# A hand-planned order of steps for a four-layer gated block, laid out anew around the value products and scores of three attentions

## The chip, the cores and the metric

The kernel runs on one core of one Trainium2 chip. The metric is the device time of one execution in microseconds; lower is better.

## The reference

Sixteen sequences of 256 tokens with 256 features pass through four layers. Each layer adds a gated cross- or self-attention and a gated feed-forward part to x; every part reads a layer-normalised x:

```python
x = x + jnp.tanh(g_xattn[0]) * _L0_xattn_ref(_layernorm(x, axis=-1), ctx_1024, ...)
x = x + jnp.tanh(g_ffn[0]) * _L0_ffn_ref(_layernorm(x, axis=-1), ...)
x = x + jnp.tanh(g_xattn[1]) * _L1_xattn_ref(ctx_1024, _layernorm(x, axis=-1), mask_BxS2_bk1, ...)
x = x + jnp.tanh(g_ffn[1]) * _L1_ffn_ref(_layernorm(x, axis=-1), ...)
...
```

The attentions that matter here are the one of layer 0 (32 score heads of width 8, two of them sharing one value head of width 16), the one of layer 2 (16 heads of width 16) and a third one inside the feed-forward part of layer 2 (16 heads of width 8). All three have this form:

```python
scores = jnp.einsum('bhtd,bhsd->bhts', q * scaling, k)
attn_w = jax.nn.softmax(scores.astype(jnp.float32), axis=-1).astype(scores.dtype)
...
attn = jnp.einsum('bhts,bhse->bhte', attn_w, v)
```

The rest: layer 0's feed-forward part applies three cycles of a small coupling network, each cycle reading the result of the one before it; layer 1 has a masked attention with 8 heads of width 64 over 512 keys and a mixture of ten experts; layer 2's mixture has eight experts; layer 3 has a one-head attention and a quantised two-matrix feed-forward.

## The kernel before

**Work.** Two sequences are in flight at a time, one in each of two slots of buffers (`SLOTS = 2`), so the 16 sequences take 8 passes. For each sequence the work is cut into named steps: `l0.q` is the query projection of layer 0, `l0.max`, `l0.exp` and `l0.pv` are parts of its attention, `f0` is the feed-forward part of layer 0, `f2` that of layer 2, and so on. A step has a part on some of the engines: TensorE fills a tile in PSUM, and ScalarE or VectorE reads it.

**An attention of the spread kind (layers l0, l2 and f2).** A unit is two heads. For unit u,
- `max` (line 625): TensorE computes scores, four matmuls that contract over 32 rows (64 in l2) of the array; VectorE takes their maximum (line 1243);
- when all units of the sequence have a maximum, `peak` and `shift` put the negated maxima into extra rows of the queries (line 558 on TensorE, line 1262 on VectorE);
- `exp` (line 642): TensorE computes the scores again, transposed and shifted, and ScalarE takes the exponential (line 975) into one of two buffers `pt_spread` of the slot (`EXPS = 2`), so ScalarE must wait until the value product two units back has read its buffer;
- `pv` (line 709): TensorE multiplies values by these probabilities. Each head writes 32 output rows and so uses 32 columns of the array, chosen by `tile_position=(0, g)`. The profile shows eight matmuls for a `pv` step, since each product in f32 runs as two.
- after every second unit (each item) ScalarE copies the result out of its bank `o` (line 913), and after four items TensorE transposes them back (`back`, line 721).

Which quarter of the array a unit uses follows from its number. In l0 and f2 an even unit's scores use rows 0 to 63 and an odd unit's rows 64 to 127, with the parity swapped in the odd slot (`u ^ (s % 2)`); a unit's value product uses the lower or the upper 64 columns in the same way. Two adjacent steps of one kind with different halves are called complementary below. In l2 a unit's scores use both halves of the rows, and only the value products have halves.

**PSUM.** Six banks are handed round (`placed_in_banks`) to all steps but `pv`, in the order of the steps; `max` and `exp` take two each, so only three such tiles are alive at a time. `take` makes TensorE wait until the step that held the banks last was read. Two further banks hold the value products.

**The order.** A single list of steps, `SCHEDULE`, sets the order on TensorE, VectorE, ScalarE and GpSimd alike: each of them walks the list and does its parts. The list is written out by hand as a string: every letter of `ORDER` names one of 24 lists (12 for each slot) of which the next step is to be taken, and each list keeps the right order among its own steps.

```python
lists = [iter([step for p in range(PASSES) for step in lists_of(p * SLOTS + n // LISTS)[n % LISTS]]) for n in range(LISTS * SLOTS)]
found = [next(lists[int(n, 36)], None) for n in ORDER]
return [step for step in found if step]
```

A step that comes too early in this list blocks its engine, since engines don't overtake; one that comes late delays what needs it. The feed-forward part f0 is a chain within a sequence: `t` (line 769 on TensorE) gives the coupling, VectorE's `turn` (line 1320) applies it, and `cT` (line 558) transposes the result for the next cycle.

Of the kernel before, what the change touches and what calls it, by code (L numbers as in the profile page):

```python
# [214 lines left out]
def lists_of(s):  # L215
# [14 lines left out]


ORDER = (
    "DAM11ADM11ADDAAMAAAA7AAAJAMAAAAAAAMA1AMMAMAD0M050M50M505M0M50M50M50M5M0550M50M50M5M0M505M0M55CC5HC0HCHCHCHCHC2H0CH0CHHC0"
    "HCHCHCH0CHC60HHE2607H606C002JC0C0C00CI0CIC00IC0CI0EC00CC200C0CC0CEC0C0C0CBC0EB0B0C00C5B0B0C500550B0C55B00CC5CB0N0C50NCC5"
    "NCCNHCNCHCNCHCC5H0HCNN007CHCCHHC3H0H0C30C093009C08980C968689C6CCCL6LCKIC8K6LCKLKL0I9KI08I9CIL068C9J09860L83698660CCKLKCI"
    "LI0KK0LII0KIC00F0C0FF00FC00000C00C00C505AC0C50C50C5C0C50C5C5C5C07C0CCHC0HCH0H00C0000CH00HC000C0H0H0H00C0JAC00055CCC0CCCC"
    "C05CC05C0C5C0C50C5C5CC4C57C04CC0HC0H0C0HCMHCHCHC0HHH0BCJ1CCGCC0G9DCB1CC8L0K69BCLI809K6CLI8BK60CI9LB8K069BC8L069KI8B6CI01"
    "L91K8BIA069CL8AA6K0ACILMADAK0D0ICDJA0ADA0AM0C7AA0MM1C0AA0CAC0AAAAA0AAM0C0MC0M50M50C505050M5CM0M50M50MCM550M50M50M50M5MMM"
    "CM050MCCC55HCH5C0HCHCHC2HCHCHC0HHCH0C7HC0HCHCH06C2EH6H06HC060002C0CC000C0ICIC00IC0CI00E0C00J2C0ECC0CCC0C0C0CBC0E0B0CB0CB"
    "C0500B500C550B0C55B00CC5CB00NC50NCC5NCCNHCNCH5CCHH70HCNCN0CCHCNCH0HC3H0H0CJ03C30F09090C898096C68869CCCLC6LCKCKL8KIL0I9IK"  # L240
# [32 lines left out]
    "C505C05C0C50C5C0C50C5C5C57C0C00CCHCHCH0C000000H00CH0C000HCH0H0H0JC00C00C055C0CCCCCC05CC05C0C5CC05C0C5CC5C45C0CC0H0CH0CHC"
    "H0CHCHCHHJ0H0CCGCCC0G9CCC8LK0I6C9L8K0C69I8LKC06IL9K8IC6L0K98CI60LK9I80C69L8K069I7CL8604KI0C00C0C0CC00CC0C0C0CC0C"
)


# [1561 lines left out]
```

How the kernel before makes its waits and increments, by code:

```python
        def full(eng, step, s, u=0):  # L479
            eng.wait_ge(S["s_wfull"], UNIT[step, s, u])
            return bank_of(step, s, u)
# [63 lines left out]
            def take(step, s, u=0):  # L546
                for last in BANKS[step, s, u][2]:
                    pe.wait_ge(*after(READ[last[0]], READER.get(last[0], last[0]), *last[1:]))
                return bank_of(step, s, u)
# [37 lines left out]
            def spread_attention(plan, what, s, u):  # L588
                st = plan.name
                if what in ("k", "q"):
                    act = ctxT[s] if what == "k" and plan is not F2 else x0T[s] if plan is L0 else xnT[s]
                    if what == "k" and plan is not F2:
                        pe.wait_ge(*after("s_ctxT", "ctxT", s))
                    else:
                        pe.wait_ge(*after("s_xnT", st + ".xT", s))
                    weight = mat({"l0": "l0_w", "l2": "l2_w", "f2": "f2_"}[st] + what, FC)
# [2 lines left out]
                    act, name = (xnT[s], "f2_v") if plan is F2 else (ctxT[s], st + "_wv")  # L599
                    filled(by_tokens(take(st + ".v", s), act, mat(name, FC), P if plan is F2 else D, FC))
                elif what in ("ks", "qs"):
                    w = take(st + "." + what, s, u)
                    pe.wait_ge(*after("s_lo", st + "." + what[0], s))
                    pe.wait_ge(s_select, 1)
                    sel = {32: {"q": sel8q, "k": sel8k}, 64: {"q": sel16q, "k": sel16k}}[plan.rows][what[0]]
# [301 lines left out]
        @block.scalar  # L908
        def _(act):
            act.wait_ge(s_first, 16)
```

## Time and profile before

| | |
|---|---|
| median of 3 runs | 4502.43 us (4487.78 to 4503.43) |
| span of the profiled execution | 4493.2 us |
| TensorE matmul busy | 4197.2 us (93%) |
| VectorE busy | 2949.1 us (66%) |
| ScalarE busy | 2085.8 us (46%) |
| mean granted TensorE clock | 0.972 |

The span runs from the first to the last instruction of the program in one profiled execution. No separate time of that execution is recorded beside its span; what lies around the span is taken as the difference to the median, 9.2 us. The profile's busy share of an engine counts the time in which at least one of its instructions runs.

### The profile page before, as it was taken

To read this page: it belongs to the slowest core of one execution; us is meant where nothing else is said; L and a number is where in the kernel's file an instruction comes from. 1 tells how busy PE (TensorE), PEld (TensorE's weight loads), DVE (VectorE), ACT (ScalarE), POOL (GpSimd) and SP (SyncE) were. 2 spreads that over 40 slices of the span, in tenths; PEclk is the share of its full clock that TensorE was granted. 3 is DMA by queue.
4 is the path that set the end of the run, shared out by engine and by line. 5 is a ranking of instruction groups with operands and counts; after the bars stand their busy time and mean duration, and the time that the engine had idled before them with its cause. 6 is when DMAs were issued, how large, how long until landed. Compare 5 with 4: busy or idle time off the path is not lost.

```text
span 4493.2 us, 73928 instructions
## 1 busy us (share of the span) xinstructions
PE 4197.2 (93%) x28256; PEld 3198.6 (71%) x28256; DVE 2949.1 (66%) x7812; ACT 2085.8 (46%) x3424; POOL 91.9 (2%) x180
## 2 busy tenths in 40 slices
PE   7898998989989899898999999999999999999998
PEld 4675966759667596675966759667696676956768
DVE  6667776676656666666765767657676576665655
ACT  4544455353553435535355353553535535356342
POOL 0000000000000000000000000000000000000000
PEclk8999999999999999999999999999999999999999
DMA  2010610103001030010300103001030010300012
GB/s 99 1 45 10 217 37 1 52 23 132 29 15 41 24 128 29 15 41 29 123 29 15 41 29 123 29 15 41 29 123 29 15 41 29 123 29 15 31 55 102
DMA packets 51769, 228.06 MB, mean 51 GB/s; under 512 B 4832, under 2 KB 21216, under 8 KB 31584
## 3 DMA queue, kind: packets, MB, share of 16 engines
q1 hardware_dynamic: 51424, 223.33, 13.8%
q8 instruction: 232, 3.80, 0.3%
q14 instruction: 113, 0.93, 0.1%
HBM read 202.34 MB, written 20.97 MB: 50 GB/s over the span
## 4 chain that ended last, share of the span: by engine, by line
PE 80%; DVE 12%; ACT 5%; issue 3%; DMA 0%; SPq 0%; DVEq 0%; ACTq 0%
PE w L574 18%; PE w L584 12%; PE o L709 11%; PE w L830 8%; PE w L820 8%; PE w L642 4%; PE w L558 4%; PE o L702 3%; DVE mx L1243 3%; PE w L625 3%; PE w L677 2%; PE w L567 2%; PE w L721 1%; DVE nt L1184 1%; PE w L612 1%
## 5 line engine op out<-in xcount | busy, mean ns | idle before, releaser
L1243 DVE TENSOR_REDUCE mx<-w 128x4 f32<-128x1024 f32 x512 | 606.8, 1221 | 180.5 <-PE w L625 167.2
L975 ACT ACTIVATE pt_spread<-w 128x1024 f32<-128x1024 f32 x512 | 519.9, 1024 | 236.8 <-PE w L642 203.7
L709 PE MATMUL o<-pt_spread,va 128*32 128x256 f32 x4096 | 543.2, 396 | 30.5 <-ACT pt_spread L975 29.8
L921 ACT ACTIVATE oth<-w,res 128x256 f32<-128x256 f32 x656 | 276.9, 471 | 569.4 <-PE w L820 470.3
L574 PE MATMUL w<-xnT,stream 128*128 128x256 f32 x1792 | 413.1, 382 | 1.4 <-ACT xnT L913 0.8
L574 PEld LDWEIGHTS w<-xnT,stream 128*128 128x128 f32 x1792 | 338.2, 191 | 50.7 <-DVE x L1212 1.0
L709 PEld LDWEIGHTS o<-pt_spread,va 128*32 128x32 f32 x4096 | 205.0, 111 | 202.2 <-issue 63.3
L820 PE MATMUL w<-qodd,va_hi 128*128 128x256 f32 x2048 | 344.8, 283 | 1.1 <-issue 0.8
L820 PEld LDWEIGHTS w<-qodd,va_hi 128*128 128x128 f32 x2048 | 284.6, 188 | 7.8 <-issue 2.4
L1502 DVE TENSOR_REDUCE mx<-w 128x2 f32<-128x1024 f32 x128 | 155.8, 1225 | 199.2 <-PE w L679 198.9
L1212 DVE SCALAR_TENSOR_TENSOR x<-w,gate,x 128x256 f32<-128x256 f32 x512 | 223.2, 477 | 90.6 <-PE w L830 71.7
L642 PEld LDWEIGHTS w<-qsp,ksp 32*128 32x128 f32 (+1 forms) x2048 | 151.0, 187 | 173.7 <-issue 139.7
L625 PE MATMUL w<-ksp,qsp 32*128 32x256 f32 (+1 forms) x2048 | 232.6, 339 | 36.3 <-DVE mx L1243 17.7
L642 PE MATMUL w<-qsp,ksp 32*128 32x256 f32 (+1 forms) x2048 | 245.5, 328 | 20.3 <-DVE qsp L1262 18.3
L702 PE MATMUL o<-pt,va 128*65 128x256 f32 x1024 | 238.8, 379 | 0.1
L625 PEld LDWEIGHTS w<-ksp,qsp 32*128 32x128 f32 (+1 forms) x2048 | 147.0, 197 | 124.1 <-issue 57.2
L574 PE MATMUL w<-xnT,res 128*128 128x256 f32 x768 | 211.6, 419 | 18.9 <-ACT xnT L913 14.5
L913 ACT ACTIVATE oth<-o 128x256 f32<-128x256 f32 (+1 forms) x384 | 146.7, 382 | 169.0 <-PE o L709 92.9
L820 PE MATMUL w<-qodd,stream_lo 128*128 128x256 f32 x1024 | 204.8, 282 | 0.0
L1084 ACT ACTIVATE oth<-w 128x256 f32<-128x256 f32 x160 | 61.3, 383 | 303.0 <-PE w L574 287.6
L1184 DVE SCALAR_TENSOR_TENSOR nt<-rs,ve 128x1 f32<-128x1 f32 x1056 | 184.5, 216 | 18.8
L913 ACT ACTIVATE pt<-w 128x1024 f32<-128x1024 f32 (+1 forms) x144 | 140.6, 976 | 113.2 <-PE w L567 95.6
(263 smaller groups left out, 7722.5 us busy)
## 6 DMA issues: line engine op xcount, KB each, us to landing
stream_lo<-split SPq DMA_DIRECT2D x56, 1024.0 KB, 4.8
va_hi<-split SPq DMA_DIRECT2D x56, 1024.0 KB, 6.9
stream<-in_moe_dram SPq DMA_DIRECT2D x80, 384.0 KB, 3.1
stream<-in_resident_dram SPq DMA_DIRECT2D x8, 2048.0 KB, 7.4
raw<-in_moe_dram SPq DMA_DIRECT2D x8, 1024.0 KB, 6.8
split<-va_hi SPq DMA_DIRECT2D x8, 1024.0 KB, 8.9
split<-stream_lo SPq DMA_DIRECT2D x8, 1024.0 KB, 10.8
stream<-in_resident_dram SPq DMA_DIRECT2D x8, 1024.0 KB, 4.7
```

The lines of the kernel that those rows point to most:

```text
L574: mm = pe.matmul(w[:, col0 + j * T:col0 + j * T + T], weight[:, k, (m0 + j) * P:(m0 + j + 1) * P], act[:, k, :], start=(k == 0), stop=(k = ...
L584: mm = pe.matmul(w[:, o:o + n], act[:, k, tt * P:(tt + 1) * P], weight[:, k, :], start=(k == 0), stop=(k == kc - 1))
L625: mm = pe.matmul(w[:, a * 512 + tt * T:a * 512 + (tt + 1) * T], qsp[s][b:b + plan.rows, c, tt * P:(tt + 1) * P], ksp[s][b:b + plan.rows, c ...
L642: mm = pe.matmul(w[:, a * 512 + kt * T:a * 512 + (kt + 1) * T], ksp[s][b:b + plan.rows, c, kt * P:(kt + 1) * P], qsp[s][b:b + plan.rows, c ...
L702: mm = pe.matmul(o[0:L1_DIM + 1, 0:T], by_heads1(s)[:, kt, u, :], p[:, kt * T:(kt + 1) * T], start=(kt == 0), stop=(kt == KT - 1))
L709: mm = pe.matmul(o[g:g + 32, 0:T], by_heads(plan, s)[:, kt, plan.v_of(h), :], p[:, a * 512 + kt * T:a * 512 + (kt + 1) * T], start=(kt == ...
L820: mm = pe.matmul(w[:, j * T:(j + 1) * T], wt[:, k, j * P:(j + 1) * P], a[:, k, :], start=(n == 0), stop=(n == len(parts) - 1))
L830: mm = pe.matmul(w[:, tt * D:(tt + 1) * D], a[:, k, tt * P:(tt + 1) * P], wt[:, k, :], start=(n == 0), stop=(n == len(parts) - 1))
L913: act.activation(out_ap, in_ap, ACT.Copy).then_inc(S[sig], 1)
L921: h = act.activation(dst[:, c, :], w[:, c * T:(c + 1) * T], func, bias=bias[:, c:c + 1], **more)
L975: act.activation(exp_buffer(plan.name + ".exp", s, u), w[:, :], ACT.Exp, scale=scale).then_inc(S["s_P"], 1)
L1243: dve.tensor_reduce(mx[s][:, :, 2 * v:2 * v + 2].rearrange("p t a -> p a t"), w[:, :].rearrange("p (a t k) -> p a t k", a=2, t=TT), AX_X, ...
```

## The change

Only the string `ORDER` changes. It has the same letters, each as often as before (5032), so the same steps are done with the same instructions, and each list keeps its own order; 1476 of the steps keep their place in the common list, the others move by 2 places on average (mean of all). The banks are handed round in the new order, so a step may get other banks and wait for another step's reader.

```diff
 ORDER = (
-    "DAM11ADM11ADDAAMAAAA7AAAJAMAAAAAAAMA1AMMAMAD0M050M50M505M0M50M50M50M5M0550M50M50M5M0M505M0M55CC5HC0HCHCHCHCHC2H0CH0CHHC0"
+    "DAM11ADM11ADDAAMAAAA7AAAJAMAAAAAAAMA1AMAADM0M0M50M50M50M50M50M50M50M5M0550M50M50M50M5500MMM55CC5HCHCHC0HCHCHC0HH2CC0HHH0"
...
```

Counted over the list of TensorE's 3856 steps, with the halves as defined above:

| | before | after |
|---|---|---|
| adjacent complementary value products, in pairs | 26 | 125 |
| adjacent complementary scores (l0, f2), in pairs | 175 | 252 |
| neighbours of different kind (32-row score, 64-row score, value product, any other) | 1740 | 1535 |

The 99 new value pairs lie in l0 (35), l2 (37) and f2 (27).

The first place is on TensorE in the third pass, in layer 0 of the odd slot (`va1`), about the middle of its 16 units; `ob0` and `kvT0` belong to the even slot's projection of its result. In these rows "x4" is one step, and "x8" are two steps side by side. Before:

```order
L709 MATMUL o1<-pt_spread1_61,va1 32x256 x4
L642 MATMUL w<-qsp1,ksp1_62 128x256 x4
L558 MATMUL w<-res,ob0 128x128 x4
...
L642 MATMUL w<-qsp1,ksp1_62 128x256 x4
L721 MATMUL w<-res,oth1 128x128 x8
L584 MATMUL w<-res,kvT0_54 128x256 x4
L709 MATMUL o0<-pt_spread1_61,va1 32x256 x4
```

After:

```order
L558 MATMUL w<-res,ob0 128x128 x4
L721 MATMUL w<-res,oth1 128x128 x8
L709 MATMUL o0<-pt_spread1_61,va1 32x256 x8
L642 MATMUL w<-qsp1,ksp1_62 128x256 x8
L584 MATMUL w<-res,kvT0_54 128x256 x4
L709 MATMUL o1<-pt_spread1_61,va1 32x256 x4
```

Two value products (units 8 and 9), and after them two scores, now stand side by side; the projection of the even slot has moved behind them.

The second place is on TensorE in the same pass, in the attention of layer 2: units 3 to 7 of the even slot (`va0`) beside the maxima of the odd slot (`ksp1`). Before:

```order
L709 MATMUL o1<-pt_spread0_58,va0 32x256 x4
L625 MATMUL w<-ksp1_62,qsp1 128x256 x4
L642 MATMUL w<-qsp0,ksp0_59 128x256 x4
L625 MATMUL w<-ksp1_62,qsp1 128x256 x4
L709 MATMUL o0<-pt_spread0_58,va0 32x256 x4
```

After:

```order
L709 MATMUL o1<-pt_spread0_58,va0 32x256 x4
L642 MATMUL w<-qsp0,ksp0_59 128x256 x4
L625 MATMUL w<-ksp1_62,qsp1 128x256 x8
L709 MATMUL o0<-pt_spread0_58,va0 32x256 x8
L642 MATMUL w<-qsp0,ksp0_59 128x256 x4
```

Two maxima of the odd slot stand together, and the value products of units 4 and 5 are one pair behind them.

The third place is on TensorE in the fourth pass, in the feed-forward part f0: the even slot's `t` of cycle 1 (line 769) and the transpose `cT` of cycle 2 (line 558 of `xt0`), which needs what VectorE makes of it. Before:

```order
L769 MATMUL w<-res,oth0 128x1 x2
L574 MATMUL w<-xnT1,res 128x256 x4
L746 MATMUL w<-gsm1,res 128x1 x2
L574 MATMUL w<-oth1,res 128x256 x2
L558 MATMUL w<-res,xt0 128x128 x4
```

After:

```order
L769 MATMUL w<-res,oth0 128x1 x2
L574 MATMUL w<-xnT1,res 128x256 x4
L558 MATMUL w<-res,xt0 128x128 x4
L574 MATMUL w<-oth1,res 128x256 x2
L746 MATMUL w<-gsm1,res 128x1 x2
```

Between the two steps of the even slot stood three steps of the odd slot before, and stands one now.

## Rows read from the trace of the kernel before

**Rows 1.** The page's head and its busy times by engine.

```profile
span 4493.2 us, 73928 instructions
PE 4197.2 (93%) x28256; PEld 3198.6 (71%) x28256; DVE 2949.1 (66%) x7812; ACT 2085.8 (46%) x3424; POOL 91.9 (2%) x180
```

**Rows 2.** Span and mean granted clock by core.

```profile
core 0: 4493.2 us, clock 0.972
```

**Rows 3.** The page's costliest groups: out<-in, count, busy us, mean ns, idle before.

```profile
L1243 DVE TENSOR_REDUCE mx<-w 128x4 f32<-128x1024 f32 x512 | 606.8, 1221 | 180.5 <-PE w L625 167.2
L975 ACT ACTIVATE pt_spread<-w 128x1024 f32<-128x1024 f32 x512 | 519.9, 1024 | 236.8 <-PE w L642 203.7
```

**Rows 4.** Timeline of TensorE, third pass, layer 0: start us, us, instruction, count.

```profile
1199.07 1.09 PE L709 MATMUL o<-pt_spread,va 128*32 128x256 f32 x16
...
1203.79 0.50 PE L642 MATMUL w<-qsp,ksp 32*128 32x256 f32 x4
1204.22 1.06 PE L709 MATMUL o<-pt_spread,va 128*32 128x256 f32 x8
1205.21 0.50 PE L642 MATMUL w<-qsp,ksp 32*128 32x256 f32 x4
1205.64 1.06 PE L709 MATMUL o<-pt_spread,va 128*32 128x256 f32 x8
```

**Rows 5.** The same timeline, earlier in the stage: complementary scores.

```profile
1165.93 0.38 PE L642 MATMUL w<-qsp,ksp 32*128 32x256 f32 x2
1165.94 0.39 PE L625 MATMUL w<-ksp,qsp 32*128 32x256 f32 x2
...
1166.38 1.06 PE L709 MATMUL o<-pt_spread,va 128*32 128x256 f32 x8
1167.37 0.38 PE L642 MATMUL w<-qsp,ksp 32*128 32x256 f32 x2
...
1167.98 1.06 PE L709 MATMUL o<-pt_spread,va 128*32 128x256 f32 x8
```

**Rows 6.** Timeline of TensorE's weight loads (PEld) for the first row of rows 4.

```profile
1199.07 0.61 PEld L709 LDWEIGHTS o<-pt_spread,va 128*32 128x32 f32 x16
```

**Rows 7.** Waits of TensorE: waited for, us in total, times, longest us.

```profile
PE o L709 <- ACT pt_spread L975: 29.8, 31, 1.7
PE w L642 <- DVE qsp L1262: 18.3, 20, 1.5
PE w L625 <- DVE mx L1243: 17.7, 37, 2.0
...
PE w L558 <- DVE ob L1320: 16.5, 7, 3.0
...
PE w L625 <- ACT qsp L913: 7.8, 9, 2.2
```

**Rows 8.** Stretches of the third pass: us, busy by engine, PEclk, DMA.

```profile
1163.00:1230.00 67.00, 66.41 (x567) 40.59 (x565) 44.45 (x111) 45.38 (x64) 2.16 (x3) 1.00 0.14 48
1230.00:1300.00 70.00, 59.18 (x243) 41.84 (x241) 43.35 (x146) 30.66 (x58) 2.10 (x3) 0.90 0.00 1
...
1474.00:1516.00 42.00, 37.04 (x296) 22.45 (x292) 29.71 (x80) 24.22 (x32) 0.94 (x2) 0.92 0.01 2
1516.00:1567.00 51.00, 46.41 (x365) 29.44 (x362) 33.75 (x79) 26.35 (x40) 0.99 (x3) 0.97 0.11 42
```

**Rows 9.** Timeline of TensorE in f0, third pass: `t`, then `cT`.

```profile
1251.66 0.57 PE L769 MATMUL w<-res,oth 64*128 64x1 f32 x4
...
1255.83 0.63 PE L558 MATMUL w<-res,xt 128*128 128x128 f32 x4 [0.26 <-DVE xt L1320]
```

More of the change, by code:

```diff
@@ L237 @@
[L237 to L240, printed above, removed]
@@ L273 @@
[L273 to L274 removed]
+    "DAM11ADM11ADDAAMAAAA7AAAJAMAAAAAAAMA1AMAADM0M0M50M50M50M50M50M50M50M5M0550M50M50M50M5500MMM55CC5HCHCHC0HCHCHC0HH2CC0HHH0"
+    "CCHCHCH0CHC0HH260EH06066C02C07C000CC00CE0ICI0ICI0C0C0CC200CC0CJ0CEC0C0C0CB0CB00B500B5C0B05C00E05CB0C55B00CCC50B0NC50NCCN"
@@ new lines @@
+    "5CNC7HCNCHCCNHC5CHC0HNCN0HCHC0HC3H0H0C03C3009J900C898906C89668CCCCLLCK6KLCII86CKIL09CKL0KI089L6I80C6980LK989863I660CKCLI"
+    "CL0K0LKKIII0C00F0FCC00F00F0000C0C000C5A050CC50C50CC550C0CC5C55C0C0CC7HC0HH00C0C0000HH00C0C0H0C00HH0H0JC00C0005C5CAC0CCCC"
+    "C0CC550CCC0C55C0C0CC55C5C0CC00HCHCMHC7HCBHHCC40HHHC40C0CC0CB0CGJ9CC8L60K9B8IC0L6KC19L8IB6K09ICGBML8D60K9C8LIBKI1069CLD86"
+    "B11KIA0AA9CALAA8BAK670I9CLA8D60K1IAC00D0AA0M0JA0CD0MMCAA0CCA0AAAA0AAAM0C0MC0505050CM50M50M50MM550M5C050MCM55M0M0M50M50M5"
@@ new lines @@
+    "M0MCMMCCC552HHCC5H0CHCHCHCHCHCH0HHCC0HC0HCHCH0C606HH0H06C207602C0CC000C00IC0CI0ICIE0C0E0C20C00ECC0CCC0C0C0JCB0CE0B0CBCC0"
+    "B050BC0500550B50C50B0CCC50BN0C50NCC5NCCNHCNCHCH5CHC0HNN0CC7CHHCNC033CHH0H0C033C0F0909C08908C8969668CCCCLCL6K8IKLCK6ICL0K"
+    "908ILI9K6J80609I8096C988LCKC660LCI00KLKIIL0CLKK0IIC0F0C00F00FC0000C0C000C5A050CC50C50CC550C0CC5C55C0C0CC0AH7CHC00HH00000"
+    "C00C00HHC0C00HH0H0C00JC00055CC0CC0CCCC55CC0C0C5C0C5C0CCC554C5C740CC0HHCCM00HCH0CHCHC10HH0H1CGCC11CCAJ0CG9CCL8KCA6I0LA9KI"
@@ new lines @@
+    "AA8DACL0K96I86AACL09KI8AC6L09KI86AA0C9L86KIAA0C9LA8A6AKI09MAA86C0DL0ADA0KI0C0DMJ0D0CMCM07CCA0AC0MC0C1MM000M50M50M50M50M5"
+    "0M50M50M5M0550M50M50MC50MCMMCM5500CCC55HHCC5H02CHCHCHCHCHC07HHHCC0HCHCH0CH06CE0HH60H0620C602C0C00C0C00C0CII0ICI0C0E0J2C0"
+    "0C0ECC0CCC0C0C0CBC0ECB00BC005B0CB0C500550B505C0B0CC5C0B0NC50NCC5NCN7CHCNCHCCH5HCH0NNC0CCHHCNC03HC3H0HJ30C009C30090890C88"
+    "9696F6C8CCCL6CL8CK6KIILCLKC0K0L9IK90I8C908LI086969688C6K6C0LC0LKIK0ILI0CLKKI00ICFF0C0000F0C000C0C000C505MC0C5C050CC550C0"
@@ new lines @@
+    "C00C0CII0ICI0C0C0002C0ECC0CCC0C0C0CBC0CBC00JB500E0CCB505CB00CCC50N5CB05CB00HN05CB50CN0CNHCC5NCCHNCC5HCH0NNC0HC0CH3C7HH0H"
+    "3C300C090F90C08989066C889CC6CCLLC6KCKILL8I6KCLK0908IKC9II80CL6900JL9689883C666C0KKL0K0LIII0CKLK0IICF0000F00F0C00C0C0C000"
+    "C5050CC50C50CC550C0CC55C5C0C0CCHC0HH07C00C0000HH00C0C0H0C00HH0JH000CC000C55CC0C0CCCC55CC0C0C5C0C50CCC55C4C5C0CC0HCH7CHCH"
+    "CHC0HC0HHH0CC0CCC009CCC8L6K0C9I8LKGJI069CL86KC0LI9K8ICL06K98CI0L6K98G06I9CL8K609IC8L60K00IC4C00C0CC00CC00CC0CC0C"
```

59 lines of the change are left out of this document (24 added, 35 removed).

## The prediction

> **What bounds the kernel now.** I read the page first, then the stretches of one pass, then TensorE's waits, and last its timeline. TensorE has a matmul running in 4197.2 of 4493.2 us, VectorE in 2949.1 and ScalarE in 2085.8 [rows 1]. So TensorE's own work is the length of the kernel, plus the 296 us in which it stands idle; on the whole the other two have room. By stage this differs. In the attention of layer 0 (1163 to 1230) TensorE is busy 66.4 of 67.0 us, VectorE 44.5 and ScalarE 45.4. In f0 (1230 to 1300) TensorE is idle for 10.8 of 70 us, in the attention of layer 2 (1474 to 1516) for 5.0 of 42 and in that of f2 (1516 to 1567) for 4.6 of 51 [rows 8]. There a shorter TensorE step can turn into a longer wait. The waits that concern the moved steps are: value products for ScalarE's exponentials, 29.8 us in 31 waits; scores for a bank that VectorE's maximum still reads, 17.7 in 37; the first `exp` of an attention for the shifted queries, 18.3 in 20, with 1.5 the longest; the transpose of f0 for VectorE's turn, 16.5 in 7; the first `max` for the spread queries, 7.8 in 9 [rows 7].
>
> **What a pair is worth.** A value product alone takes from 1204.22 to 1205.21, 0.99 us from its start to the next step's; a lone score takes 0.43 (1203.79 to 1204.22). Two complementary value products run as one block of 16 matmuls in 1.09 us [rows 4]. That saves 2 x 0.99 - 1.09 = 0.89 us per pair. The reader is to see that the second step costs 0.1 us, not nothing and not 0.5. For scores the timeline shows the mixing itself: `exp` of one slot and `max` of the other come as two and two, 0.01 us apart. One pair takes 0.45 us (1165.93 to 1166.38), the next 0.61 (1167.37 to 1167.98), and both kinds alternate [rows 5]. The mean is 0.53 against 0.86 alone, so 0.33 us saved; the bounds are 0.25 and 0.41.
>
> The order gives 99 more value pairs and 77 more score pairs. So 99 x 0.89 = 88 us and 77 x 0.33 = 25 us, 113 us of TensorE time in all. Its bounds: if no new pair overlapped, 0; by the better score price, 88 + 32 = 120. I take 113, since 26 value pairs and 175 score pairs of the same kinds stand in the order already, and the blocks that I priced are two of them.
>
> The Trainium skill speaks against the first term: "TensorE: Matmul & The Clock Gate", section on packing small matmuls, says that a weight load overlaps running matmuls only when its row group is another one, and the loads of two value products both use all rows. By that rule the value pairs would save next to nothing, and the sum would be 25 us. The trace of this kernel doesn't agree: in that block of 16 matmuls all 16 loads lie within the first 0.61 us or so of a block in which the matmuls never pause [rows 4, 6].
>
> **What the new order takes back.** Before a step waits it needs lead: other TensorE work between what it depends on and itself. I laid the lengths above along both orders and counted where the lead is too short, four kinds of place.
>
> Value products: a `pv` needs ScalarE's exponential, 1.02 us [rows 3], about 1.1 after its scores, and 2.1 after them where two `exp` stand side by side. In a pair, the second exponential must be ready 0.46 us after the pair begins. Places that fall short go from 39 to 78, and the missing lead from 24 to 34 us; the trace's 29.8 us of such waits [rows 7] fits the 24. That is 10 us more.
>
> Banks: only three two-bank tiles live at a time, and a `max` needs 1.22 us on VectorE, an `exp` 1.02 on ScalarE [rows 3]. Places that come to their banks under 1.3 us after the last `max` was issued there go from 63 to 101, under 1.1 us after an `exp` from 11 to 45; missing lead 25 to 55 us. These stand in the same runs as the places above, and one wait serves both, so I take half of the 30, 15 us, with bounds 0 and 30.
>
> First steps of an attention: in the even slots of layer 2 the first `exp` now follows the last `shift` with nothing between, where 0.7 us of work stood. With nothing between the wait is the longest of its row, 1.5 us [rows 7], so 8 x 0.7 = 6 us more. The first `max` of f2 has 0.2 to 0.4 us ahead of it in 13 slots, where 1.4 us stood; the row of such waits has a mean of 0.87 us [rows 7], so about 13 x 1.1 = 14 us at most. In seven slots of layer 2 the same lead grows from under 0.8 to over 1.3 us, which gives about 5 back. Net 9 us.
>
> f0: from the start of `t` to its `cT` the shortest way is 4.2 us (1251.66 to 1255.83), 3.6 of it after `t` ends [rows 9]. Of the 32 such places 15 have less than 3.6 us of work between, in both orders, but what is missing goes from 6 to 20 us. The third place shown in the change is one of them: three steps between became one. 14 us more. A bound from the other side is 0: the longest such waits now, 3.0 us [rows 7], stand where the lead is above 4 us and VectorE is late for other reasons, and these may shrink.
>
> Together 10 + 15 + 6 + 9 + 14 = 54 us, with bounds of about 10 (only the value products, which the trace bears out) and 110 (twice as much, if each late step makes the next one late too). The other work moves by a place or two and is costed at nothing: its instructions are the same, and its cover is the TensorE work around it. If that cover were gone, it would show in the same kinds of waits. DMA queues are not passed, since their waits are on steps that move by a few microseconds.
>
> **Sum.** 113 - 54 = 59 us off the profiled span of 4493.2, so 4434; the median of the runs stands 9.2 us above that span, and I keep this: 4502.4 - 59 = 4443 us.
>
> **Rivals.**
> - More comes through. If the leads that I miss are found by work that I count as idle (TensorE is idle 296 us in any case), the gain is 95 to 113 us, 4389 to 4407 us. For it: in layer 0, where 35 value pairs stand, TensorE waits for next to nothing and both other engines have a third of the time free [rows 8]. Against: 37 pairs stand in layer 2, where VectorE's chain of maxima, 8 x 1.22 = 9.8 us for a slot, is as long as TensorE's work beside it.
> - The pairs don't overlap in practice. Two steps mix only if both are released when the first begins. If ScalarE's second exponential is late in half of the new value pairs, 44 us are lost from the gain, and 113 - 44 - 54 = 15 us are left: 4487 us, no change that can be told. For it: 48 + 12 of the 125 pairs have under 1.0 us between the second `exp` and the pair. Against: 1.1 - 0.46 = 0.64 us is enough for most of them.
> - Slower through the clock. The mean granted clock is 0.972 [rows 2]; as the levels are 1.0 (2.4 GHz) and 0.5 (1.2 GHz), 5.6% of the span, 252 us, runs at the lower one. Those stretches lie where TensorE idles: 0.90 in f0 and 0.92 in layer 2, 1.00 in layer 0 [rows 8]. If the added waits stretch them, work there takes twice as long. The gain of 59 us is gone when 118 more microseconds run at 1.2 GHz, 15 in each pass, which would be a mean clock below about 0.959. With twice that, the kernel takes 4561 us. Against: value pairs pack more matmuls into the same time in exactly these stages.
> - Slower because value pairs gain nothing: 25 - 54 us, so 4531 us. The 1.09 us block speaks against it directly [rows 4].
>
> **How the numbers follow.** The forecast, with a gain of 25 to 90 us, has 0.63. The larger gain has 0.18. Late partners, or waits at twice my sum, leave a change within 22 us: 0.12. Slower through the clock 0.06, slower through pairs without worth 0.01. Half a per cent, 22 us, is about what a measurement of this kernel can tell from none. Faster by over 0.5%, under 4480 us, is 0.63 + 0.18 = 0.81; within it 0.12; slower 0.07. The range that holds 8 in 10 leaves out the slower cases and the upper edge of the middle ones, and at the bottom what lies under the full gain: 4390 to 4488 us. The likeliest case alone spans 4412 to 4478.
>
> **What would show it.** In the profile of the changed kernel TensorE's busy time falls by 90 to 115 us, and its idle time rises by 30 to 80. In the timeline line 709 comes in rows of x16 about 125 times, 1.09 us each. In the waits view the rows for `pt_spread`, for `mx` before line 625 and 642, and for `qsp` before lines 642 and 625 grow by 10 us or so each, and line 558 waits longer for line 1320. VectorE's and ScalarE's busy times stay within 1%. I am wrong if TensorE's busy time falls by less than 70 us (pairs that don't overlap), if idle time grows by more than 90 us, or if the clock's mean leaves 0.965 to 0.98.

## The result: 0.4% slower where 1.3% faster was forecast

| | before | after |
|---|---|---|
| median, 9 runs each | 4494.63 us | 4513.29 us |
| ratio, 95% interval | | 1.0036 [1.0024, 1.0048] |
| profiled span | 4493.2 us | 4511.5 us |

The order laid out anew makes the kernel slower, by 0.24 to 0.48%. This is within the 0.5% that counts as no change in the chances, but above the 4480 us under which most of the chance lay, and above the range, which ended at 4488. In the profile of after, the page's head and busy times [as rows 1] and the clock [as rows 2] are:

```profile
span 4511.5 us, 73892 instructions
PE 4159.7 (92%) x28256; PEld 3198.5 (71%) x28256; DVE 2949.2 (65%) x7812; ACT 2081.9 (46%) x3426; POOL 91.8 (2%) x180
```

```profile
core 0: 4511.5 us, clock 0.961
```

TensorE's busy time falls by 37.5 us, not by 90 to 115, and its idle time (span less busy) grows from 296.0 to 351.8 us. The clock falls from 0.972 to 0.961. The waits of TensorE, which answer to [rows 7] (waited for, us in total, times, longest us), and then the page's row of the value products (busy, mean ns | idle before):

```profile
PE w L642 <- DVE qsp L1262: 26.8, 21, 1.5
PE w L625 <- DVE mx L1243: 24.9, 47, 2.1
PE w L558 <- DVE ob L1320: 22.2, 12, 3.3
PE o L709 <- ACT pt_spread L975: 21.6, 37, 1.2
...
PE w L574 <- ACT xnT L913: 16.1, 32, 1.0
...
PE w L625 <- ACT qsp L913: 9.5, 15, 1.3
```

```profile
L709 PE MATMUL o<-pt_spread,va 128*32 128x256 f32 x4096 | 467.9, 407 | 22.3 <-ACT pt_spread L975 21.6
```

Against before, the first row has grown by 8.5 us, the second by 7.2, the third by 5.7 and the last wait by 1.7. The wait of the value products for ScalarE, which was to grow by 10, has fallen by 8.2. In the page of before the same row of line 709 read:

```profile
L709 PE MATMUL o<-pt_spread,va 128*32 128x256 f32 x4096 | 543.2, 396 | 30.5 <-ACT pt_spread L975 29.8
```

So value products do run in less time together, 75 us less, and the mean of one is no shorter: they overlap, as they should in pairs. But not every pair is a short block. Of the rows of x16 in after, 70 take 1.09 to 1.13 us; 29 more at 2.4 GHz take 1.2 to 2.3 us, 14 us in all above 1.09 each (9 rows and 6 us in before). One of these 29 (TensorE, then ScalarE):

```profile
669.34 1.89 PE L709 MATMUL o<-pt_spread,va 128*32 128x256 f32 x16 [0.17 <-ACT pt_spread L975]
```

```profile
668.17 1.94 ACT L975 ACTIVATE pt_spread<-w 128x1024 f32<-128x1024 f32 x2 [2.52 <-PE w L642]
```

The second exponential ends at 670.11, and the second product starts at 670.16. This lateness counts as TensorE's busy time, not as a wait, as the first product is still running.

**Where the time went.** Two things hide in "busy": work, and the stretches in which the same work runs at 1.2 GHz. I took them apart by laying every step of TensorE in the trace beside the granted clock. A step's time runs from its start to the start of the next, less idle time. *Work* is that time with what lies at 1.2 GHz counted half; *clock cost* is the rest of it; *waits* is TensorE's idle time between and within steps. The three add up to the span but for 6.1 us in both traces, at its ends.

| | waits | work | clock cost | us at 1.2 GHz |
|---|---|---|---|---|
| before | 291.8 | 4082.1 | 113.2 | 253 |
| after | 347.6 | 3996.3 | 161.5 | 355 |
| difference | +55.8 | -85.8 | +48.3 | +103 |

The sum is +18.3 us, the difference of the two spans. The forecast was +54, -113 and 0. The page "TensorE: Matmul & The Clock Gate" of the Trainium skill, section "Terms", reckons the penalty as the throttled time multiplied by the share of clock pulses that are held back, a half here. My clock cost is made by that same rule (on busy time alone), so the 48 us for 103 don't test it. Two other numbers do: a lone value product takes 1.86 us to the next step's start at 1.2 GHz and 0.99 at 2.4, and i3_leads_after below, with 27 us more of clock cost than after, comes out with the same work within 1 us (3996.9 beside 3996.3).

Each step's three terms can also be added up by the stage that it belongs to, over both slots and all passes. This shows where the net loss is:

| stage | waits | work | clock cost | net |
|---|---|---|---|---|
| layer 0's attention | +11.3 | -33.9 | -0.2 | -22.8 |
| f0 | +5.2 | -1.0 | +5.0 | +9.2 |
| layer 1's attention | +1.7 | -0.3 | -6.0 | -4.6 |
| layer 2's attention | +0.1 | -25.2 | +18.9 | -6.2 |
| f2 | +36.1 | -25.6 | +30.1 | +40.6 |

All others together are within 4 us. Layer 0 gained, though less than its pairs were priced at; the steps of f2 (its attention, its router and its experts) lose more than the whole kernel does.

The cost of the clock can be seen in the timeline of TensorE in after, third pass, attention of f2 (start us, us, instruction, count):

```profile
1553.38 1.09 PE L709 MATMUL o<-pt_spread,va 128*32 128x256 f32 x16
...
1557.68 1.10 PE L709 MATMUL o<-pt_spread,va 128*32 128x256 f32 x8
...
1560.06 1.93 PE L709 MATMUL o<-pt_spread,va 128*32 128x256 f32 x8
1561.92 0.58 PE L642 MATMUL w<-qsp,ksp 32*128 32x256 f32 x2
```

The first row is a pair at 2.4 GHz. The second is a lone product at 2.4 GHz but for its end, and the third another one, in a stretch of 10.2 us at 1.2 GHz that begins at 1558.6. The slow one takes 1.86 us to the next step's start (the fourth row) where 0.99 is usual: one product at 1.2 GHz costs 0.87 us more, about what a pair saves (0.89). By stages, the stretches of the third pass show where this happens (us, busy by engine, PEclk, DMA). These are layer 0's attention, f0, layer 2's and f2's attention, each from its first step of the even slot (the first `exp` for an attention) to the first of the next stage. Before:

```profile
1163.20:1222.80 59.60, 59.09 (x509) 35.44 (x508) 39.72 (x91) 39.51 (x54) 2.16 (x3) 1.00 0.15 54
1222.80:1297.20 74.40, 63.50 (x287) 45.48 (x286) 46.69 (x165) 35.12 (x66) 2.10 (x3) 0.91 0.00 1
1473.70:1528.30 54.60, 47.51 (x374) 29.82 (x374) 41.05 (x96) 28.10 (x38) 1.83 (x4) 0.94 0.01 1
1528.30:1579.90 51.60, 48.82 (x378) 32.18 (x379) 27.25 (x81) 30.15 (x48) 0.20 (x2) 0.97 0.17 62
```

After:

```profile
1187.50:1245.80 58.30, 57.17 (x521) 34.86 (x520) 40.59 (x91) 40.16 (x55) 2.09 (x3) 1.00 0.16 55
1245.80:1313.20 67.40, 55.42 (x275) 40.61 (x274) 46.62 (x165) 34.15 (x65) 2.09 (x3) 1.00 0.00 1
1489.20:1543.00 53.80, 46.59 (x370) 30.73 (x370) 40.52 (x96) 25.09 (x35) 1.78 (x4) 0.87 0.00 1
1543.00:1596.90 53.90, 50.58 (x383) 33.82 (x383) 27.42 (x81) 30.48 (x49) 0.20 (x2) 0.87 0.16 60
```

The clock of the last two falls from 0.94 and 0.97 to 0.87. That of f0 rises from 0.91 to 1.00 here, but over the eight passes f0 has 51 us at 1.2 GHz after 68 before. The attentions of layer 2 and f2 have 147 after 72, and layer 1's attention and f2's experts 36 after none.

### The profile page after: what moved, and what is told of

Same layout as the page of the kernel before. It is cut to its first block, busy times and chain, and to the rows that moved or that the text cites. A ratio compares the mean times of both kernels' runs of the same rounds, so it can differ in the third digit from the quotient of the medians.

```text
span 4511.5 us, 73892 instructions
## 1 busy us (share of the span) xinstructions
PE 4159.7 (92%) x28256; PEld 3198.5 (71%) x28256; DVE 2949.2 (65%) x7812; ACT 2081.9 (46%) x3426; POOL 91.8 (2%) x180
## 4 chain that ended last, share of the span: by engine, by line
PE 69%; DVE 13%; ACT 5%; issue 3%; DVEq 0%; POOL 0%; ACTq 0%
PE w L574 15%; PE w L584 11%; PE w L820 8%; PE w L830 8%; PE o L709 7%; PE o L702 3%; DVE mx L1243 3%; PE w L558 3%; PE w L642 3%; PE w L567 2%; PE w L677 2%; PE w L625 2%; PE w L612 1%; DVE nt L1184 1%; PE w L721 1%
## 5 line engine op out<-in xcount | busy, mean ns | idle before, releaser
L709 PE MATMUL o<-pt_spread,va 128*32 128x256 f32 x4096 | 467.9, 407 | 22.3 <-ACT pt_spread L975 21.6
L709 PEld LDWEIGHTS o<-pt_spread,va 128*32 128x32 f32 x4096 | 186.9, 113 | 169.4 <-issue 67.5
L642 PE MATMUL w<-qsp,ksp 32*128 32x256 f32 (+1 forms) x2048 | 234.8, 335 | 31.8 <-DVE qsp L1262 26.8
L574 PE MATMUL w<-xnT,res 128*128 128x256 f32 x768 | 217.8, 429 | 18.3 <-ACT xnT L913 15.3
L574 PEld LDWEIGHTS w<-xnT,res 128*128 128x128 f32 x768 | 156.1, 213 | 56.2 <-issue 24.3
## 6 DMA issues: line engine op xcount, KB each, us to landing
split<-stream_lo SPq DMA_DIRECT2D x8, 1024.0 KB, 11.3
```

The source lines that it names most:

```text
L574: mm = pe.matmul(w[:, col0 + j * T:col0 + j * T + T], weight[:, k, (m0 + j) * P:(m0 + j + 1) * P], act[:, k, :], start=(k == 0), stop=(k = ...
L642: mm = pe.matmul(w[:, a * 512 + kt * T:a * 512 + (kt + 1) * T], ksp[s][b:b + plan.rows, c, kt * P:(kt + 1) * P], qsp[s][b:b + plan.rows, c ...
L709: mm = pe.matmul(o[g:g + 32, 0:T], by_heads(plan, s)[:, kt, plan.v_of(h), :], p[:, a * 512 + kt * T:a * 512 + (kt + 1) * T], start=(kt == ...
```

## The experiments

The table has, for each, the ratio to before with its 95% interval, and the three terms of its profiled execution as above (one execution, which can lie some us off the median); for kernels with filler matmuls the time of the filler is counted as waits.

| kernel | ratio | waits | work | clock cost |
|---|---|---|---|---|
| before | 1 | 291.8 | 4082.1 | 113.2 |
| after | 1.0036 [1.0024, 1.0048] | 347.6 | 3996.3 | 161.5 |
| e1_l0 | 1.0039 [1.0027, 1.0052] | 332.4 | 4048.0 | 134.0 |
| e2_l2f2 | 1.0027 [1.0018, 1.0036] | 312.6 | 4030.7 | 163.3 |
| e3_rest | 1.0139 [1.0121, 1.0158] | 332.3 | 4086.8 | 139.8 |
| e4_split_l2f2 | 1.0138 [1.0119, 1.0157] | 357.5 | 4046.6 | 151.6 |
| e5_split_l0 | 1.0106 [1.0089, 1.0122] | 338.8 | 4029.0 | 163.6 |
| e6_split_all | 1.0211 [1.0189, 1.0233] | 348.0 | 4080.1 | 155.3 |
| i3_leads_after | 1.0128 [1.0112, 1.0145] | 364.0 | 3996.9 | 188.4 |
| g1_pairs_l0 | 0.9997 [0.9987, 1.0008] | 303.3 | 4063.2 | 128.4 |
| g2_pairs_l2f2 | 1.0020 [1.0010, 1.0030] | 316.4 | 4049.4 | 134.7 |
| h1_three_before | 1.0001 [0.9991, 1.0010] | 291.1 | 4081.9 | 113.2 |
| h2_three_after | 1.0050 [1.0036, 1.0064] | 344.4 | 3994.7 | 172.4 |
| h3_three_g1 | 0.9966 [0.9952, 0.9979] | 299.4 | 4061.0 | 112.2 |
| i2_pairs_all_three | 0.9944 [0.9930, 0.9958] | 315.7 | 4026.8 | 128.9 |
| f1_fill_before | 0.9917 [0.9902, 0.9931] | 354.2 | 4057.7 | 36.1 |
| f2_fill_after | 0.9928 [0.9913, 0.9944] | 424.4 | 3976.1 | 44.5 |
| i1_fill_h3 | 0.9880 [0.9865, 0.9896] | 360.2 | 4034.4 | 42.2 |
| j1_fill_i2 | 0.9878 [0.9861, 0.9894] | 382.5 | 4004.5 | 42.1 |

### Parts of the new order, stage by stage

Three kernels take the new order in some stages and keep the old one in the others; like the change itself, they differ from before in `ORDER` alone. In the diffs of orders, here and below, a row is a step of TensorE in the common list, with its sequence and its unit. From e1_l0 (layer 0's attention and the end of a pass), e2_l2f2 (the attentions of layer 2 and f2) and e3_rest (all other stages, 4 new value pairs), against before:

```diff
 l0.exp 8 2
+l0.max 9 4
 l0.pv 8 1
+l0.max 9 5
 l0.exp 8 3
...
 f2.exp 7 7
+ctxT 8 0
+f2.cTr 6 0
 f2.pv 7 6
-f2.cTr 6 0
-ctxT 8 0
 f2.pv 7 7
...
 l2.shift 4 0
+l2.qs 5 0
 l2.shift 4 1
-l2.qs 5 0
 l2.exp 4 0
```

> The order of before, with the new order only in the stretches around the attention of layer 0 and the end of a pass: 32 more value pairs and 37 more score pairs, all in layer 0. Theory 'clock' (pairs are worth what they were priced at, but in the attentions of l2 and f2 and around them TensorE then runs longer at 1.2 GHz): layer 0 has no stretch at 1.2 GHz, so it keeps 32 x 0.89 + 37 x 0.33 = 40 us less about 12 us of waits, so about 28 us faster than before, with a mean clock of 0.970 to 0.974. Theory 'waits' (the pairs' worth is eaten by waits for ScalarE and VectorE wherever they stand): at most 10 us faster, idle time up by 25 or more.

> The order of before, with the new order only around the attentions of layer 2 and f2: 37 + 26 more value pairs and 30 more score pairs. 'Clock': 66 us of pairs, less about 20 of waits, less about 40 for 80 more microseconds at 1.2 GHz: within 15 us of before, mean clock 0.961 to 0.966. 'Waits': the clock stays at 0.970 or above, and idle time grows by 40 us or more.

> The order of before, with the new order only in f0, layer 1, f1, the steps between f1 and the attention of layer 2, and the experts of f2: nearly no new pair. 'Clock': these moves buy nothing and cost 10 us of waits and 20 to 30 us at 1.2 GHz, so 10 to 25 us slower than before, mean clock about 0.968. 'Waits': 20 to 40 us slower with the clock unchanged at 0.972.

Measured: 4521.8, 4514.62 and 4566.42 us beside 4500.88 of before. Each part alone is slower than before, and the part with nearly no pairs most of all. In e1_l0 waits rise by 41 us, as theory 'waits' had it; e2_l2f2 fits theory 'clock', with 50 us more of clock cost and a clock of 0.960; e3_rest, 66 us slower, fits neither. The three do not add up to the whole: 21 + 14 + 66 us against some 19. A mix hands the banks round in a third way, since a step's banks follow from its place in the whole list, and so it can hold waits that neither order has. So these runs don't locate the loss: in e1_l0 layer 0's own steps are 18 us faster by their three terms, and f0, layer 1, layer 2 and f2, whose order is mostly the old one, lose 38. In e3_rest it is f2's steps again that lose most, 42 us. How much is due to the mixing stays open. The splits below keep the whole order, so I rely on them.

### The new order without its pairs

Two kernels are the changed order with the new value pairs of layer 2 and f2 (55), or of layer 0 (32), split by one other step; the third has all of them split, and 38 of its 125 pairs left. One place of e5_split_l0, against after:

```diff
 l0.pv 6 8
+l0.exp 6 10
 l0.pv 6 9
-l0.exp 6 10
 l0.exp 6 11
```

> The order of after, with 55 value pairs of layer 2 and f2 taken apart again (the second product one TensorE step later, nothing else moved); 11 score pairs of f2 go with them. 'Clock': TensorE has 49 + 4 us more to do, but the time at 1.2 GHz falls by 60 to 75 us, which gives 35 back: 10 to 25 us slower than after, mean clock 0.967 or above. 'Waits': the clock stays at 0.961 and the kernel is 35 to 53 us slower than after.

> The changed order with the value pairs of layer 0 that are new split again by one score step between their two products; the other pairs stay. Theory 'ring': in layer 0 the two buffers hand the pair's gain back as waits for the exponential, so splitting costs less than 15 us: 4505 to 4528 us. Rival 'pairs pay in full': 0.89 us for each, some 30 us slower than after: 4535 to 4555 us.

> The changed order with the new value pairs of all three attentions split again by one score step (38 of 125 are left), so that it keeps the new order's other moves. Theory 'the waits are the order's, not the pairs'': TensorE's work at full clock returns to that of before (some 4080 us), while idle time stays at 335 to 360 us, 45 to 65 above before, and the time at 1.2 GHz stays above 320 us: 4570 to 4600 us. Rival 'the pairs make the waits': idle time falls back by 30 us or more, to 315 us or less, and with it the time at 1.2 GHz toward 254: 4500 to 4540 us.

Measured: 4564.93, 4540.79 and 4591.3 us. The last one is what decides. Its page's head, clock and first waits:

```profile
span 4589.5 us, 73892 instructions
PE 4237.4 (92%) x28256; PEld 3228.7 (70%) x28256; DVE 2949.0 (64%) x7812; ACT 2088.6 (46%) x3426; POOL 91.7 (2%) x180
```

```profile
core 0: 4589.5 us, clock 0.963
```

```profile
PE w L625 <- DVE mx L1243: 31.1, 54, 2.3
PE w L642 <- DVE qsp L1262: 27.2, 21, 1.7
PE w L558 <- DVE ob L1320: 19.8, 11, 3.2
```

With nearly all new pairs gone, the work is back at 4080.1 us (4082.1 before), but the waits are 348.0, as with the pairs (347.6), and the clock cost is 155.3 against 161.5. So the change falls into two parts. From before to this kernel, its other moves cost 96 us of span: 56 of waits, 42 of clock, and -2 of work. From this kernel to after, the pairs give 78 us back: 84 of work and nothing in waits, less 6 of clock cost. In this order the pairs do not make the waits. By stage the other moves lose 65 of their 96 us in f2's steps (41 of waits, 23 of clock, 2 of work). Split stage by stage, the 55 pairs of layer 2 and f2 are worth 50 us of span (4561.7 - 4511.5), and the 32 of layer 0 26 us (4537.5 - 4511.5). The splits take 11 and 28 score pairs along, so by the forecast's prices they should be worth 53 and 38. In layer 0 the work is 33 us more, but waits are 9 less (4.9 of them at `l0.pv`). So waits take a part of these pairs' gain, not most of it as my theory had it, and they need not be the ring's: with a third buffer (h2_three_after below) `l0.pv` waits 6.2 us, the same as in after. Nor did e4_split_l2f2 go as theory 'clock' had it: the time at 1.2 GHz fell by 27 us and not by 60 to 75.

### Giving the first steps their lead back

> The changed order with its pairs kept, but 46 first steps of a chain (14 transposes cT of f0, 12 first maxima of f2, 8 first exp of layer 2, 5 first maxima of layer 0, 4 first exp of f2, 3 of layer 1) moved back behind the TensorE steps of the other slot that stood before them in the order of before, up to three of them. Theory 'first steps': a good part of the 56 us of added waits stands at these steps (in the trace of after, f2.max 13.9 us, f0.cT 9.8, l2.exp, l1.exp and l0.max about 5 each, f2.exp 4.6 more than before), so idle time falls by 20 to 40 us and with it some of the time at 1.2 GHz: 4460 to 4490 us. Rival 'moved on': the waits are the shape of the data flow and only move to the next step, idle time falls by under 10 us and the time stays within 15 us of after, 4500 to 4525.

```diff
 f0.h1 5 0
+f0.h2 5 0
 f0.cT 4 2
-f0.h2 5 0
 f0.g1 5 0
...
-l0.max 6 0
 f2.down 5 1
 ctxT 7 0
+l0.max 6 0
 l0.max 6 1
```

The kernel moves less than the expectation says: in TensorE's order 21 steps stand later than in after, not 46, by one or two places (10 `f0.cT`, 6 `f2.max`, 3 `l0.max`, one `l1.exp`, one `f2.exp`, and no `l2.exp`). So it gives only some of the first steps their lead back.

Measured: 4556.0 us, 43 more than after, above both ranges. The rival was right that the waits only move on, but had them as harmless. In the trace, `f0.cT` waits 19.1 us in place of 26.6 and `f2.max` 17.4 in place of 20.0; `f0.h1` rises from 11.0 to 20.8, `f0.h2` from 13.1 to 18.6 and `l1.max` from 0.9 to 8.0. In the waits view it is this row that has grown, from 16.1 us in after:

```profile
PE w L574 <- ACT xnT L913: 25.6, 40, 2.4
```

Waits are 16 us longer and the clock costs 27 more (0.955). So what depends on the steps that I moved back waits in its turn. Whether a version that moves all 46 would do the same was not run.

### Pairs alone, in the old order

The other way round: before, with value products joined by moving the first one behind up to three steps of other kinds, 28 pairs in layer 0 (g1_pairs_l0) and 48 in layer 2 and f2 (g2_pairs_l2f2). A place of each:

```diff
+l0.exp 5 10
 l0.pv 5 8
-l0.exp 5 10
 l0.pv 5 9
...
 f2.exp 7 7
-f2.pv 7 6
 f2.cTr 6 0
 ctxT 8 0
+f2.pv 7 6
 f2.pv 7 7
```

> The order of before with 28 of the new value pairs of layer 0 and nothing else: in each the first product is put off, past one to three TensorE steps, to stand just before the second. 'Worth': a pair saves 0.89 us wherever TensorE is the bound, so 25 us less TensorE work, about 5 us of waits, 15 to 25 us faster than before, clock at 0.972. 'Ripple' (what the first mixed kernel suggests: in this order any local move of work costs waits and clock elsewhere that outweigh it): within 5 us of before or slower, idle time up by 20 us or more in stretches where nothing was moved.

> The order of before with 48 of the new value pairs of layer 2 and f2 and nothing else, 12 score pairs arising from it. TensorE has 43 + 4 us less to do. 'Pairs lower the clock': about 10 us of waits, and 60 to 80 us more at 1.2 GHz in these stages, 30 to 40 us of loss: within 10 us of before, clock 0.960 to 0.966. 'The clock follows the other moves, not the pairs': clock stays above 0.969, 30 to 40 us faster than before.

Measured: 4496.74 and 4506.06 us beside 4495.39. Work falls by 19 and 33 us, and waits and clock cost take all of it back, and in the second kernel somewhat more (12 and 15 us in the first, 25 and 21 in the second). For a part of the waits in layer 0 the timeline of g1_pairs_l0 shows how; TensorE first, then ScalarE in the same microseconds:

```profile
1221.43 1.09 PE L709 MATMUL o<-pt_spread,va 128*32 128x256 f32 x16
1222.45 0.50 PE L642 MATMUL w<-qsp,ksp 32*128 32x256 f32 x4
1223.78 1.06 PE L709 MATMUL o<-pt_spread,va 128*32 128x256 f32 x8 [0.82 <-ACT pt_spread L975]
```

```profile
1218.51 1.02 ACT L975 ACTIVATE pt_spread<-w 128x1024 f32<-128x1024 f32 x1
1222.61 1.02 ACT L975 ACTIVATE pt_spread<-w 128x1024 f32<-128x1024 f32 x1 [3.09 <-PE o L709]
```

ScalarE stands idle for 3.09 us until the pair has read its buffers. Both buffers of the slot are held by the two products of the pair, so the next exponential starts only when the pair ends, and the next value product waits 0.82 us, nearly the 0.89 that the pair saved.

### A third buffer for the exponentials

The ring gets a third buffer, laid over a tile (`turned2`) that is free in these stages:

```diff
-            return pt[:, n % EXPS, :] if ring == 0 else pt_spread[s][:, n % EXPS, :]
+            if ring and n % 3 == 2:
+                return turned2[s][:, :, :].rearrange("p t k -> p (t k)")
+            return pt[:, n % EXPS, :] if ring == 0 else pt_spread[s][:, n % 3, :]
...
-                if n >= EXPS:
-                    last, ls, lu = EXP_STEPS[ring][n - EXPS]
+                held = 3 if ring else EXPS
+                if n >= held:
+                    last, ls, lu = EXP_STEPS[ring][n - held]
```

> The order of before with three buffers instead of two for the exponentials of l0, l2 and f2 (the third lies over the odd probability buffer of layer 1, idle then). 'Ring' (a value product that is put off to stand beside the next one holds its buffer, so ScalarE starts the exponential two units on late, and the pair gives its gain back as a wait): in the order of before products follow their exponentials at once, so a third buffer changes little, 0 to 5 us faster. 'Any move ripples': the same, no difference.

> The order of after with the third buffer. 'Ring': TensorE's waits for pt_spread and for banks whose exponential is late shrink by 15 to 25 us, and the kernel is 15 to 30 us faster than after, at 4485 to 4500. 'Any move ripples' (the waits come from the other moves of the order, not from the buffers): within 5 us of after.

> The order of before with only the 28 value pairs of layer 0, as run before with two buffers (no difference to before), now with the third buffer. 'Ring': the pair in layer 0 no longer holds ScalarE up, the 16 us of waits that it brought go, and the kernel is 15 to 22 us faster than before (ratio 0.995 to 0.9965). 'Any move ripples': still within 5 us of before.

> The order of before with 76 more value products of layer 0, layer 2 and f2 joined into pairs (nothing else moved), and three exponential buffers for each slot in place of two. Theory 'ring and clock': the pairs of layer 0 are worth their 0.6 us each, as 28 of them with the third buffer gave 15 us, while the 48 of layer 2 and f2 are eaten by the maxima's waits and more time at 1.2 GHz: 4470 to 4492 us. Rival 'the ring alone': with the third buffer all pairs are worth 0.5 to 0.9 us: 4425 to 4450 us.

Measured: on before 4487.86 us beside 4487.39 (nothing); on the pairs of layer 0 4472.23 us, 0.34% faster where the same pairs on two buffers gave nothing; on all 76 joined pairs 4471.9 us, 0.56% faster. On after 4511.45 us, a ratio of 1.0050 where after has 1.0036: no gain. In h2_three_after the waits are 344.4 us, 3 less than in after. So the third buffer makes pairs pay that are pushed into the old order, but the ring is not what the new order loses by. The traces of g1_pairs_l0 and h3_three_g1 say that the ring's own share is small: `l0.pv` waits 6.2 us with two buffers and 1.4 with three, all waits fall by 4 us (not by the 16 expected) and work by 2, and the other 16 of the 22 us between the two spans are clock cost. Why the clock falls less often there is not shown.

### Holding the clock

To see what the clock is worth, matmuls of no use are put into the waits: each writes a bank that the step behind it fills anew. f1_fill_before has 1444 of them in 214 waits, f2_fill_after 1668 in 229, i1_fill_h3 1496 in 224 and j1_fill_i2 1512 in 226:

```diff
+            def fill(bank, step, s, u):
+                for _ in range(FILL.get((step, s, u), 0)):
+                    pe.matmul(bank[:, 0:T], sel8q[:, 0, :], sel8q[:, :, :].rearrange("p a b -> p (a b)"), start=True, stop=True)
...
+                fill(bank_of(step, s, u), step, s, u)
                 return bank_of(step, s, u)
```

> The order of before with 1444 matmuls added at 214 places at which TensorE waits for data by the trace: each writes 256 columns of the tile that the waiting step is about to overwrite, reads nothing that is late, and takes 0.11 us, so that 162 us of waiting are filled and no result depends on them. 'Clock': the time at 1.2 GHz falls from 254 us to 150 or less, and the kernel gets 30 to 60 us faster. 'Clock doesn't matter' (work at 1.2 GHz lies where VectorE or ScalarE is the bound, so it costs little): the clock rises, but the time stays within 10 us or grows by the fillers that come too late.

> The order of after with 1668 such matmuls at its own 229 places, 187 us of waiting filled. 'Clock': the time at 1.2 GHz falls from 357 us to 200 or less, and 50 to 80 us come off after's time; the new order with fillers then beats the old one with fillers by 10 to 35 us, the 89 us by which its TensorE work at full clock is shorter less the 56 us by which it waits longer. 'Clock doesn't matter': within 15 us of after.

> The kernel with 28 joined pairs in layer 0 and a third exponential buffer, with 1496 matmuls of no use put into 224 waits of TensorE (they write a bank that the step behind them fills anew). Theory 'clock and ring add up': the fill was worth 38 us on the order of before and pairs with the third buffer 15 us, together 4440 to 4450 us beside 4495 of before, the fastest kernel here. Rival 'the clock has already paid': the 15 us came from less time at 1.2 GHz, which the fill gives anyway, so 4453 to 4462 us, no better than the fill alone.

> 76 joined value pairs, three exponential buffers and 1512 matmuls of no use in 226 waits. Theory 'all three add': against the kernel with pairs in layer 0 alone and the fill (4442.6 us), 48 more pairs take some 20 to 30 us of work and the maxima's waits give back as much as they did without the fill, 24 us in all over before: 4425 to 4443 us. Rival 'only the clock hid it': the waits cost as much as the pairs save, as with the fill on the changed order: 4443 to 4460 us.

Measured: 4457.3 us, 4463.29, 4442.64 and 4437.03. The head and clock of f2_fill_after, whose clock is to be read beside after's 0.961:

```profile
span 4451.2 us, 77068 instructions
PE 4272.4 (96%) x29924; PEld 3348.7 (75%) x29924; DVE 2946.5 (66%) x7812; ACT 2083.4 (47%) x3426; POOL 92.1 (2%) x180
```

```profile
core 0: 4451.2 us, clock 0.987
```

On the changed order the filler takes the time at 1.2 GHz from 355 to 114 us and the kernel gains 50 us. That shows that the waits let the clock fall: the steps and their order are the same. It does not make the new order the better one, as I had expected. With the clock held, f2_fill_after has 82 us less work than f1_fill_before, 70 us more waits and 8 more of clock cost, and the two spans are 3 us apart; by its median the new order is 6 us slower (the intervals 0.9917 [0.9902, 0.9931] and 0.9928 [0.9913, 0.9944] overlap). Without filler its gain but for the clock was 30 us; here 14 more of waits and filler, 8 of clock cost and 4 less of saved work take 27 of that away. (Work reads 24 and 20 us less with filler than without on the same steps, so waits and work are not cleanly parted at the filler's end; the spans and medians are what counts.) Pairs with a third buffer and the filler add up: i1_fill_h3 is 15 us faster than the filler alone by its median, 11 by its span (-23 of work, +6 of waits, +6 of clock). The 48 further pairs of j1_fill_i2 bring 30 us less of work and 22 more of waits; its ratio, 0.9878 [0.9861, 0.9894], can't be told from 0.9880 [0.9865, 0.9896]. Both beat before by 1.2% and are the fastest kernels here.

## Why the prediction was wrong

**The price of a pair was nearly right.** On average a new value pair saved 0.82 us of work (81 / 99) and not 0.89, with the late second products, one of the rivals of the prediction, counted in. The value products took 81 us less of work than before (31 in layer 2, 27 in layer 0, 23 in f2) where 88 were forecast, and the scores 18 (9.5, 5.5 and 3.0 in `l0.exp`, `f2.exp` and `f2.max`) where 25 were. The Trainium skill's rule on weight loads ("TensorE: Matmul & The Clock Gate", section on packing small matmuls), by which the first would be next to nothing, doesn't hold here. The same section's own table has three column tiles at 2.38 times the speed, so the rule alone was too narrow a reading of it. By the rule, e6_split_all would have lost 13 us of work (39 score pairs), and it lost 84.

**The sum of the first term was 27 us too high**, 113 against 86: 14 from the value products and scores, and 13 because the other steps, costed at nothing, took that much more. From after to e6_split_all the prices hold (90 us by them, 84 measured). What is missing lies in the rest of the new order: e6_split_all has 12 value pairs and 38 score pairs more than before, 23 us by the prices, and only 2 us less work.

**The take-back, 54 against 56, was right in size by luck.** Term by term, forecast and measured:

| | forecast | measured |
|---|---|---|
| value products for ScalarE's exponential | +10 | -8.2 |
| banks of the maxima and exponentials | +15 | +19.4 |
| first `exp` of layer 2 | +6 | +5.9 |
| first `max` of f2 | +14 | +7.6 |
| first `max` of layer 2 | -5 | -6.0 |
| `f0.cT` | +14 | +9.8 |
| together | +54 | +28.5 |

The banks' term is the growth of all rows of TensorE that wait for `mx` (12.0, of which 7.2 in the row of line 625) and of those before other lines than 709 that wait for `pt_spread` (7.4). The other half of the 56 us stands at steps that I hadn't counted: `f2.up` 6.0, `l1.exp` 5.2, `l2.qs` 4.5, `f2.qs` 4.3, `f2.cTr` 3.2 and others. And the reason was wrong where I wrote that a shorter TensorE step can turn into a longer wait: without the pairs the waits are the same.

**The step that failed is the clock**, which the sum had at nothing and a rival at 0.06. After has 103 us more at 1.2 GHz, which cost 48. The rival put the point of no gain at 118 more microseconds and a mean clock of 0.959. Measured were 103 and 0.961, and that was enough to lose it, as the gain without the clock was 30 us (86 - 56) and not 59. From -59 the errors lead to the result: +27 of work, +2 of waits, +48 of clock make +18. I had a price for four kinds of wait and none for what a wait does to the work behind it. One of my signs of being wrong, a mean clock outside 0.965 to 0.98, came true with 0.961. In before the 291.8 us of waits went with 113.2 of clock cost; the 56 added ones went with 48.

**My test for pairs was a wrong one.** "Busy time falls by less than 70 us: the pairs don't overlap" came true (37.5), and they overlap. Busy time holds the work at both clocks, and the 48 us hide in it.

**What stays open.** Which single wait lets the clock fall, and why some 56 us of waits let it fall so much more often (63 stretches in place of 40). Which moves in f2 make its 36 us of waits, and whether they do it by shorter leads or by the banks that the new order hands out, which no run tells apart. Waits and clock cost don't go in step from kernel to kernel: e2_l2f2 has 21 us more waits than before and 50 of clock cost, e1_l0 41 and 21. And why stage-wise mixes of the orders are slower than both was not traced to single banks.

## What to carry to other kernels

Where TensorE is near its bound and its granted clock isn't 1.00, an order of steps has three terms: work, waits, and the clock that the waits let fall; here 56 us of added waits came with 42 to 48 us of the third. Change the order only where the pair is: the 76 pairs joined on the spot with a third buffer gained 0.56%, while a whole new order with 99 more lost 0.4%. Look at the ring of buffers that a pair holds before making it, at when the second product's input is ready (a late one hides in the busy time), and at filler work in the waits, which was worth 0.8% by itself. Before trusting a sum that came out right, compare its terms: here they were right in total and off by up to 18 us each.

## What the runs showed of the hardware that I had not expected

Matmuls of no use made this kernel faster: 1444 of them, in waits, raise the granted clock from 0.972 to 0.990 and take 0.83% off the time, though TensorE then has 62 us more in waits and filler together. And moving 21 of TensorE's steps back by one or two places (i3_leads_after), with the same work to within 1 us, cost 43 us, 27 of them in the clock.
